# A graph layer's neighbour counts: two buffers of 180 nodes in turns with the products, instead of one buffer of 250

## The chip, the cores and the metric

One core of a Trainium2 chip runs the whole layer. The metric is the device time of one execution in microseconds (us). Engines are called PE (TensorE; PEld is its weight load), DVE (VectorE), ACT (ScalarE), POOL (GpSimd) and SP (SyncE, which here only issues DMAs).

## The reference, cut to what matters

There are N = 6250 nodes with D = 128 values each, and E = 206250 edges, sorted by destination (`dst`). Every edge also has 128 values of its own.

```python
msg = x[src] + edge_attr
agg = jax.ops.segment_sum(msg, dst, num_segments=N)
h = jax.nn.relu(agg @ W1 + b1) @ W2 + b2
# whole-tensor norm, norm over nodes, gelu, + x, then a layer norm of each row
```

The sum splits in two: the edges' own values, summed by destination, and `x[src]`, summed by destination. The second is a product: `agg[n] += sum_s counts[s, n] * x[s]`, where `counts[s, n]` is how many edges run from node s to node n.

## The kernel before, in words

**Stages.** (1) Set-up: `dst` and `src` are read, packed into one list in HBM (`listed`), and turned into small tables; `x` is split into two fp32r parts, `x_hi` and `x_lo`. (2) Lead rounds: groups of 3072 edges are summed by PE. (3) The chunk loop, which also sums the other groups. (4) A tail: two small matrix products per 250 nodes (`up` L740, `down` L750), the norms, and the output.

**Sums of edges.** There are 67 full groups and a rest. A group is loaded by SP in two halves of 768 KB each (L345). DVE makes one-hots for each half (`mark`, L875), PE does 24 recorded matmuls of 128 columns with 32-column weights per half (`sum_half`, L622), ACT copies the sums (`copy_sums`, L489), PE turns them (`turn_sums`, L636), and DVE adds them to `agg` (`add`, L892). Before: 8 lead rounds of 2 groups; then 2 groups in each of 25 chunks. There are 4 buffers for halves.

**Chunks.** A chunk is 250 destination nodes, taken as 125 pairs. POOL gathers for each pair the words of `listed` in which the pair's edges begin (L429, twice 128 words), DVE finds the first edge (`stage_row`, L942 to L946), POOL gathers 128 words from there (L434), DVE makes two tables from them (`make_keys`, L953 to L967), PE turns these (`turn_keys`, L656) and ACT copies them (`copy_keys`, L499). From the turned tables DVE makes marks in bf16, one batch of 25 pairs at a time, 5 batches in a chunk and 3 buffers of marks (`mark_batch`, L982, two instructions each, on 26 pairs with the padding). One matmul per pair (L672, 128 by 98) multiplies its marks into counts; 5 pairs fill a PSUM bank, 25 banks make a chunk, 3 banks go in a ring. ACT copies each bank into `counts` (L519). After the last bank of the chunk comes the product: for each of 49 tiles of nodes, `x_hi` and then `x_lo` as 128 by 128 weights and 250 columns of `counts` (L693, 98 matmuls), summed in one bank; DVE adds that to `agg` (`add_chunk`, L1034).

**Order.** Each engine runs its own list of instructions in order, and semaphores tie them. There is one buffer of counts: PE waits for ACT's last copy before the product, and ACT waits for the product before the next chunk's first copy. PE's list for chunk c is: 25 banks, with a half of a group after banks 2, 8, 14 and 20 and the next chunk's `turn_keys` after bank 20; then 98 product matmuls.

```python
if k == KEYS_AT:                                  # PE, KEYS_AT = 20
    pe.wait_ge(keys_ready, c * 2 + 2)
    turn_keys(c + 1)                              # waits for make_keys(c + 1)
...
pe.wait_ge(banks_free, (c + 1) * BANKS)
```

DVE's list for chunk c is: `stage_tile(c+1)`, batches 0, 1, 2 with the one-hots and the add of the first group between them, `add_chunk(c-1)`, `stage_row(c+1)`, batch 3, the second group, batch 4, `make_keys(c+1)`. A batch waits until the banks of the batch that had its buffer are counted (`banks_done`).

Of the kernel before, what the change touches and what calls it, by code (L numbers as in the profile page):

```python
# [14 lines left out]
P = 128  # L15
# [5 lines left out]
PER = 6  # L21
# [5 lines left out]
HALVES = 4  # L27
PLACES = 4
GPC = 2
HPC = 2 * GPC  # L30
# [11 lines left out]
CHUNK = 250  # L42
PAIRS = CHUNK // PAIR
BATCH = 25
BATCHES = PAIRS // BATCH
BP = BATCH + 1
INTER = 2
BLOCKS_B = BP // INTER
MARKED = 3
# [3 lines left out]
CREDIT = BPB + 1  # L53
RING = 3
# [4 lines left out]
KEYS_AT = 20  # L59
BURSTS = (2, 8, 14, 20)  # L60
SUMS_AT = (11, 23)
BELOW = 3
SEARCH = 13
# [7 lines left out]
def gnn_kernel(nc, x, src, dst, edge_attr, W1, b1, W2, b2, ln_w, ln_b, gn_w, gn_b, gn_ms, out):  # L71
# [11 lines left out]
    CHUNKS = N // CHUNK  # L83
    LEAD = (FULL // GPC) - CHUNKS
    LEAD0 = 2
    EVEN = GROUPS // 32 * 32
    assert D == P and 0 < REST < SUB and REST_P * PER == REST and GROUPS <= 96 and FULL == (LEAD + CHUNKS) * GPC + 1
    assert G_REST_E > G_HALF and EVEN < FULL
    assert CHUNKS * CHUNK == N and CHUNKS % 2 == 1 and LEAD > LEAD0 + 3
# [4 lines left out]
    assert PIECE * (LEAD - 1) == NT  # L94
# [5 lines left out]
    NPAIR = N // PAIR  # L100
    ROWS = E // STRIDE + 1
    LISTED = (ROWS - 1) * STRIDE + P
    assert N <= 1 << DST_SHIFT and 0 < LISTED - E <= P and LISTED % STRIDE == 0 and (ET * SPAN + P) // STRIDE < ROWS and STRIDE == 1 << 4
# [5 lines left out]
    with ExitStack() as ctx:  # L109
# [6 lines left out]
        def sem(name):  # L116
            return ctx.enter_context(nc.semaphore(name))


        edges = sb("edges", [P, HALVES, HALF * D])  # L120
# [4 lines left out]
        LW = P * BP  # L125
        KW = KEYS * BP
        pool_m = sb("pool_m", [P, max(2 * NT * D, MARKED * (LW + KW))], BF16)
        mark_lo = [pool_m[:, s * (LW + KW):s * (LW + KW) + LW].rearrange("p (b v r) -> p b v r", v=P, r=INTER)
                   for s in range(MARKED)]
        mark_key = [pool_m[:, s * (LW + KW) + LW:(s + 1) * (LW + KW)].rearrange("p (b v r) -> p b v r", v=KEYS, r=INTER)  # L130
                    for s in range(MARKED)]
        x_raw = pool_m[:, 0:2 * NT * D].bitcast(F32)
        xs = x_raw.rearrange("p (t d) -> p t d", d=D)
        behind = pool_m[:, 2 * NT * D:MARKED * (LW + KW)]
        below = behind[:, 0:BELOW * SEARCH * PAIRS].rearrange("p (s v) -> p s v", s=BELOW)

        behind_f = behind.bitcast(F32)
        lnstats = behind_f[:, 0:6 * NT].rearrange("p (t s) -> p t s", s=6)
        lnmean, lngap, rstd = [behind_f[:, k * NT:(k + 1) * NT] for k in (6, 7, 8)]
        lnmean_act = behind_f[:, 9 * NT:10 * NT]  # L140
        stats = behind_f[:, 10 * NT:10 * NT + 6 * CHUNKS].rearrange("p (c s) -> p c s", s=6)
        listing = sb("listing", [P, NPAIR + 7], BF16)
        pair_row = listing[:, :].bitcast(I16)
        values = listing[:, 0:P * INTER].rearrange("p (a v r) -> p a v r", a=1, r=INTER)
# [9 lines left out]
        place = sb("place", [P, 2, SPREAD])  # L154
# [7 lines left out]
        hidden = onehot[:, :, :].rearrange("p s e -> p (s e)")[:, 0:2 * HC * CHUNK].rearrange(  # L162
            "p (u k n) -> p u k n", u=2, k=HC)
        gelu = behind_f[:, 10 * NT + 6 * CHUNKS:10 * NT + 6 * CHUNKS + 2 * BLOCK * P].rearrange("p (u n) -> p u n", u=2)
# [9 lines left out]
        pair_i = sb("pair_i", [P, CHUNKS + 1], I32)  # L174
        pair_f = sb("pair_f", [P, CHUNKS + 1])
        pair_w = sb("pair_w", [P, CHUNKS + 1])
        tile_end_i = sb("tile_end_i", [P, SETS], I32)
        tile_end = sb("tile_end", [P, SETS])
        tile_f = sb("tile_f", [P, CHUNKS + 1])
        tile_rows = sb("tile_rows", [P, CHUNKS + 1, 2], I32)  # L180
        tile_slot = sb("tile_slot", [P, 2], I32)
# [9 lines left out]
        hi_i = sb("hi_i", [P, P], I32)  # L191
# [5 lines left out]
        turned_lo = sb("turned_lo", [P, BATCHES, BP], BF16)  # L197
        turned_key = sb("turned_key", [P, BATCHES, BP], BF16)
# [16 lines left out]
        eps = [b[:, 0:D] for b in banks[3:5]]  # L215
        turned_sum = [b[:, D:D + SPREAD] for b in banks[3:5]]
        turn_ps, sps = banks[6], banks[7]
# [3 lines left out]
        ops = [banks[4], sps, banks[0], banks[1]]  # L221
# [40 lines left out]
        pads_ready = sem("pads_ready")  # L262
# [73 lines left out]
        def _(sp):  # L336
# [11 lines left out]
            with sp.Fori(0, LEAD + CHUNKS) as r:  # L348
                for u in range(HPC):
                    load(r * GPC + u // 2, u % 2, u, r * HPC + (u + 1))  # L350
            for k in range(2):
                load(FULL - 1, k, k, 2 * (FULL - 1) + k + 1)
            sp.wait_ge(halves_free, 2 * FULL + 2)
            for k in range(2):
                sp.dma_start(edges[0:REST_P, 2 + k, 0:HP], edge_rest[:, k * HP:(k + 1) * HP]).then_inc(tail_loaded, 16)
# [47 lines left out]
        def _(pool):  # L403
            pool.iota(iota_i[:, :], [[1, P]], base=0, channel_multiplier=0)
            pool.iota(prow_i[:, :], [[0, 1]], base=0, channel_multiplier=1)
            pool.iota(pair_i[:, :], [[PAIR * PAIRS, CHUNKS + 1]], base=0, channel_multiplier=PAIR)
# [3 lines left out]
            for at, to in ((0, half), (half, NPAIR + 7)):  # L410
                pool.iota(pair_row[:, at:to], [[1, to - at]], base=at, channel_multiplier=0,
                          allow_small_or_imprecise_dtypes=True).then_inc(pair_row_ready, 1)
            for s, places in ((halves_free, HALVES), (sums_copied, 3), (sums_turned, 3), (edges_added, 2),
                              (banks_done, CREDIT), (chunk_summed, 1), (chunk_added, 1)):
                pool.sem_inc(s, places)
# [3 lines left out]
            pool.wait_ge(below_ready, 2 * SETS)  # L419
            pool.iota(listing[:, 0:P * INTER], [[1, P], [0, INTER]], base=0, channel_multiplier=0,  # L420
                      allow_small_or_imprecise_dtypes=True).then_inc(pads_ready, 1)


            with pool.Fori(0, CHUNKS + 1) as c:
# [3 lines left out]
                for k in range(2):  # L428
                    pool.indirect_dma_start(begins[0:PAIRS, k * P:(k + 1) * P], None, listed_rows,  # L429
                                            bass.IndirectOffsetOnAxis(tile_slot[0:PAIRS, k:k + 1], 0)  # L430
                                            ).then_inc(begins_loaded, 16)
# [18 lines left out]
        def _(act):  # L450
# [40 lines left out]
            def round_copies(r):  # L491
                for j in range(GPC):
                    copy_sums(r * GPC + j, j)

            def copy_keys(c):
                act.wait_ge(marks_ready, c * BATCHES)
                act.wait_ge(keys_turned, c + 1)
                for at, to in ((LO0, turned_lo), (KEY0, turned_key)):
                    nc.scalar.copy(to[:, :, 0:BATCH], turn_ps[:, at:at + PAIRS].rearrange("p (b n) -> p b n", n=BATCH)  # L499
                                   ).then_inc(keys_ready, 1)  # L500

            for g in range(LEAD0 * GPC):
                copy_sums(g, g % GPC)
            with act.Fori(LEAD0, LEAD - 2) as r:
                round_copies(r)
            act.wait_ge(pads_ready, 2)
            act.wait_ge(keys_turned, 1)
            for at, to in ((LO0, turned_lo), (KEY0, turned_key)):
                nc.scalar.copy(to[:, :, 0:BATCH], turn_ps[:, at:at + PAIRS].rearrange("p (b n) -> p b n", n=BATCH)
                               ).then_inc(keys_ready, 1)  # L510
            for r in range(LEAD - 2, LEAD):
                round_copies(r)
# [739 lines left out]
```

## Time and profile before

| | |
|---|---|
| median of 3 runs | 911.76 us (906.98 to 913.2) |
| profiled execution, its own time | 911.31 us |
| span of the profiled execution | 909.3 us |
| PE busy, PEld busy | 729.4 us (80%), 633.5 us (70%) |
| DVE busy, ACT busy, POOL busy | 678.4 us (75%), 383.4 us (42%), 145.4 us (16%) |
| mean granted TensorE clock | 0.959 |

The busy times are shares of the whole span and mix stages with different limits; what a change in the chunk loop is worth is read from one chunk. Times of instructions and stretches below are counted from the first instruction. The clock is given as a share of full speed: 1.00 is 2.4 GHz and 0.50 is 1.2 GHz. The span ends 2.0 us short of the execution's own time.

### The profile page before, as it was taken

The numbers are of one execution on the slowest core, as the hardware profiler recorded it, in microseconds if no ns is written. First come the engines' busy times: TensorE is split into PE (matmuls) and PEld (weight loads), VectorE is DVE, ScalarE is ACT, GpSimd is POOL, SyncE is SP. The second block draws the span as 40 slices with busy tenths as digits, with TensorE's granted clock in tenths as the row PEclk, the third lists the DMA queues.
The fourth block names the chain that finished last, engine by engine and source line by source line (L and its number), as shares of the span: only waits on it lengthen the run. The fifth ranks groups of instructions, "written<-read, shape, count | busy, mean of one in ns | idle before, by whom it ended". The sixth has DMA issues, their size and how long they took to land.

```text
span 909.3 us, 25887 instructions
## 1 busy us (share of the span) xinstructions
PE 729.4 (80%) x9449; PEld 633.5 (70%) x9449; DVE 678.4 (75%) x1185; ACT 383.4 (42%) x841; POOL 145.4 (16%) x91
## 2 busy tenths in 40 slices
PE   3486569888988888988889988889988889989950
PEld 2464448777877777877777877777877777877830
DVE  5844777877878877878877878877878877844576
ACT  0200034355433555433554433554434554424464
POOL 1210022120221220221120221220221220200000
PEclk9987989899999999999999999999999999999975
DMA  6669973443334443334444334443334444303004
GB/s 173 228 216 361 360 262 99 124 147 115 104 100 121 147 144 116 106 97 125 147 144 114 107 94 128 147 144 112 109 93 130 147 144 113 94 25 141 0 1 141
DMA packets 89477, 123.25 MB, mean 136 GB/s; under 512 B 9029, under 2 KB 85018, under 8 KB 89260
## 3 DMA queue, kind: packets, MB, share of 16 engines
q1 hardware_dynamic: 78992, 112.83, 39.9%
q0 software_dynamic: 6240, 5.08, 2.1%
q10 hardware_dynamic: 4228, 5.12, 1.8%
q8 instruction: 10, 0.16, 0.1%
q14 instruction: 7, 0.05, 0.0%
HBM read 118.91 MB, written 4.03 MB: 135 GB/s over the span
## 4 chain that ended last, share of the span: by engine, by line
PE 48%; DVE 26%; issue 11%; DMA 7%; ACT 5%; DVEq 2%; ACTq 1%; POOL 0%; SPq 0%; POOLq 0%
PE bank L693 33%; DVE pool_m L982 12%; DMA edges<-in_edge_attr_dram 5%; PE bank L622 3%; PE bank L672 3%; ACT counts L519 3%; DVE onehot L875 3%; PE bank L740 3%; PE bank L750 2%; PE bank L656 1%; PE bank L636 1%; DMA agg<-in_dst_dram 1%; DMA begins<-listed,tile_slot 1%; DVE node_f L965 1%; DVE node_f L957 1%
## 5 line engine op out<-in xcount | busy, mean ns | idle before, releaser
L519 ACT CAST counts<-bank 128x490 fp32r<-128x490 f32 x625 | 318.3, 606 | 324.0 <-PE bank L672 324.0
L693 PE MATMUL bank<-counts,x_hi 128*128 128x250 f32 x1225 | 293.5, 284 | 29.6 <-ACT counts L519 29.6
L693 PE MATMUL bank<-counts,x_lo 128*128 128x250 f32 x1225 | 290.6, 281 | 0.0
L982 DVE TENSOR_TENSOR pool_m<-listing,turned_lo 128x3328 bf16<-128x3328 bf16 x125 | 236.7, 1893 | 30.1 <-PE bank L672 26.7
L693 PEld LDWEIGHTS bank<-counts,x_hi 128*128 128x128 f32 x1225 | 234.8, 192 | 33.4 <-ACT counts L519 33.4
L672 PE MATMUL bank<-pool_m 128*128 128x98 bf16 x3125 | 211.2, 210 | 33.0 <-ACT counts L519 22.7
L693 PEld LDWEIGHTS bank<-counts,x_lo 128*128 128x128 f32 x1225 | 235.2, 192 | 0.0
L672 PEld LDWEIGHTS bank<-pool_m 128*128 128x128 bf16 x3125 | 161.9, 99 | 77.6 <-ACT counts L519 75.2
L982 DVE TENSOR_TENSOR pool_m<-listing,turned_key 128x2548 bf16<-128x2548 bf16 x125 | 184.5, 1476 | 0.0
L622 PE MATMUL bank<-edges,onehot 128*32 128x128 f32 x3228 | 126.7, 293 | 30.1 <-DMA edges<-in_edge_attr_dram 23.3
L429 POOL DMA_INDIRECT begins<-listed,tile_slot x52 | 101.9, 1959 | 297.1 <-DVE tile_slot L935 265.2
L622 PEld LDWEIGHTS bank<-edges,onehot 128*32 128x32 f32 x3228 | 88.8, 116 | 46.7 <-issue 20.7
L434 POOL DMA_INDIRECT begins<-listed,row_slot x26 | 33.0, 1270 | 310.6 <-DVE row_slot L946 298.4
L875 DVE TENSOR_TENSOR onehot<-iota_f,dst_cols 128x384 f32<-128x384 f32 x136 | 74.5, 550 | 1.1 <-PE bank L622 0.9
L1034 DVE TENSOR_TENSOR agg<-agg,bank 128x250 f32 (+1 forms) x25 | 10.4, 416 | 75.4 <-PE bank L693 74.6
L489 ACT COPY sums<-bank 128x128 f32<-128x128 f32 x68 | 20.2, 297 | 85.0 <-PE bank L622 85.0
L892 DVE TENSOR_TENSOR agg<-agg,bank 128x128 f32 x68 | 19.0, 280 | 39.4 <-PE bank L636 38.3
L595 PE MATMUL bank<-ones_b,pool_m 128*125 128x1 bf16 x175 | 19.2, 245 | 23.1 <-DVE pool_m L826 23.1
L595 PEld LDWEIGHTS bank<-ones_b,pool_m 128*125 128x125 bf16 x175 | 19.0, 229 | 23.3 <-DVE pool_m L826 23.3
L636 PE MATMUL bank<-place,sums 128*128 128x128 f32 x136 | 34.7, 339 | 0.4 <-ACT sums L489 0.4
L636 PEld LDWEIGHTS bank<-place,sums 128*128 128x128 f32 x136 | 21.2, 197 | 14.9 <-issue 14.0
L546 ACT ACTIVATE onehot<-bank,b1c 128x250 f32<-128x250 f32 x50 | 20.7, 466 | 25.3 <-PE bank L740 25.3
(149 smaller groups left out, 407.9 us busy)
## 6 DMA issues: line engine op xcount, KB each, us to landing
edges<-in_edge_attr_dram SPq DMA_DIRECT2D x134, 768.0 KB, 4.5
out_dram<-pool_m SPq DMA_DIRECT2D x6, 512.0 KB
begins<-listed,tile_slot POOLq DMA_INDIRECT x52, 4.2
agg<-in_dst_dram SPq DMA_DIRECT2D x1, 768.0 KB
agg<-in_src_dram ACTq DMA_DIRECT2D x1, 768.0 KB
listed<-agg ACTq DMA_DIRECT2D x1, 768.0 KB
begins<-listed,row_slot POOLq DMA_INDIRECT x26, 4.3
w<-in_L_gnn_W_dram ACTq DMA_DIRECT2D x2, 128.0 KB, 2.2
```

The costliest lines, as they stand in the source:

```text
L429: pool.indirect_dma_start(begins[0:PAIRS, k * P:(k + 1) * P], None, listed_rows, bass.IndirectOffsetOnAxis(tile_slot[0:PAIRS, k:k + 1], 0) ...
L434: pool.indirect_dma_start(near[0:PAIRS, :], None, listed_rows, bass.IndirectOffsetOnAxis(row_slot[0:PAIRS, 0:1], 0)).then_inc(near_loaded, 16)
L519: nc.scalar.copy(counts[:, :, k * nodes:(k + 1) * nodes].rearrange("p q (i m) -> p q i m", m=PAIR), cps[k % RING][:, 0:nodes * NT].rearran ...
L546: nc.scalar.activation(hidden[:, u, c, :], zps[u][:, c, 0:CHUNK], ACT.Relu, bias=b1c[:, c:c + 1]).then_inc(hidden_ready, 1)
L595: last = nc.tensor.matmul(turn_ps[0:PAIRS, c:c + 1], below[:, i % BELOW, at:at + PAIRS], ones_b[:, :], start=(c == 0 and i == 0), stop=(i ...
L622: last = nc.tensor.matmul(eps[s][b * WINDOW:(b + 1) * WINDOW, :], oh[:, t, :], edges[:, u, t * D:(t + 1) * D], start=(k == 0 and j == 0), ...
L636: nc.tensor.matmul(turned_sum[s], sums[:, :], place[:, s, :], start=True, stop=True).then_inc(sums_turned, 1)
L672: last = nc.tensor.matmul(cps[k % RING][:, i * KEYS:(i + 1) * KEYS], mark_lo[b % MARKED][:, n // INTER, :, n % INTER], mark_key[b % MARKED ...
L693: last = nc.tensor.matmul(sps[:, 0:CHUNK], part[:, q, :], counts[:, q, :], start=(q == 0 and part is x_hi), stop=(q == NT - 1 and part is ...
L740: last = nc.tensor.matmul(zps[u][:, k, 0:CHUNK], w1[:, k * P:(k + 1) * P], agg[:, bass.ds(c * CHUNK, CHUNK)], start=True, stop=True, skip_ ...
L875: dve.tensor_tensor(oh, window, of.to_broadcast([P, HALF, WINDOW]), ALU.is_equal).then_inc(onehot_ready, 1)
L982: last = dve.tensor_tensor(to[b % MARKED], values[:, :, 0:n, :].to_broadcast([P, BLOCKS_B, n, INTER]), of.to_broadcast([P, BLOCKS_B, n, IN ...
```

## The change

A chunk is 180 nodes (90 pairs, 3 batches of 30, 18 banks), so there are 35 chunks, and `counts` has two buffers. PE now goes bank by bank: it counts bank k of chunk c and then does the products of 3 tiles (6 matmuls, 180 columns) of chunk c-1, from bank 2 on (16 times 3 tiles, and one more tile at bank 17). The product's sums have a bank each for odd and even chunks. The ring of count banks has 2 instead of 3, there are 2 buffers of marks instead of 3, and 3 of edge halves instead of 4. The set-up's tables lie in the buffers of counts. Groups go 3 to a round of two chunks: a chunk has three halves, after banks 3, 9 and 15. There are 5 lead rounds of 3 groups. `turn_keys` of the next chunk comes after bank 2 instead of bank 20. Tables are prepared one chunk further ahead, and one gather of 256 words takes the place of two of 128. Chunk 0 is counted alone and the product of chunk 34 comes alone at the end. The tail keeps its 250 columns (`UP`).

```diff
-HALVES = 4
-PLACES = 4
-GPC = 2
+HALVES = 3
+PLACES = 3
+GPR = 3
...
-CHUNK = 250
+CHUNK = 180
-BATCH = 25
+BATCH = 30
-MARKED = 3
+MARKED = 2
-CREDIT = BPB + 1
-RING = 3
+RING = 2
+CREDIT = (MARKED - 1) * BPB + 1
+AHEAD = 2
-KEYS_AT = 20
-BURSTS = (2, 8, 14, 20)
-SUMS_AT = (11, 23)
+KEYS_AT = 2
+BURSTS = (3, 9, 15)
+SUMS_AT = ((11,), (5, 17))
+FIRST_Q = 2
+PER_SLOT = 3
...
-        counts = sb("counts", [P, NT, CHUNK], F32R)
+        counts = sb("counts", [P, 2, NT, CHUNK], F32R)
...
+            def multiply(par, qs):
+                for q in qs:
+                    for part in (x_hi, x_lo):
+                        last = nc.tensor.matmul(sps[par][:, 0:CHUNK], part[:, q, :], counts[:, par, q, :],
+                                                start=(q == 0 and part is x_hi), stop=(q == NT - 1 and part is x_lo))
+                if qs[-1] == NT - 1:
+                    last.then_inc(chunk_summed, 1)
+
+            def count_chunk(c, par, r, first_u):
                 for k in range(BANKS):
                     b = k // BPB
                     if k % BPB == 0:
                         pe.wait_ge(marks_ready, c * BATCHES + (b + 1))
-                    if k >= RING:
-                        pe.wait_ge(banks_free, c * BANKS + (k + 1 - RING))
+                    pe.wait_ge(banks_free, c * BANKS + (k + 1))
                     for i in range(BANK):
...
                     if k == KEYS_AT:
                         pe.wait_ge(keys_ready, c * 2 + 2)
                         turn_keys(c + 1)
+                    if r is None:
+                        continue
+                    if k == FIRST_Q:
+                        pe.wait_ge(banks_free, c * BANKS + RING)
+                        pe.wait_ge(chunk_added, c)
+                    if k >= FIRST_Q:
+                        at = (k - FIRST_Q) * PER_SLOT
+                        multiply(1 - par, range(at, NT if k == BANKS - 1 else at + PER_SLOT))
+                    if k in BURSTS:
+                        u = BURSTS.index(k) + first_u
+                        g = r * GPR + u // 2
+                        begin_half(g, u % 2, edge_loaded[u % HALVES], r * 32 + (u // HALVES * 16 + 16))
+                        sum_half(u, u // 2, u % 2)
+                        if u % 2 == 0:
+                            turn_sums(g - 1, (u // 2 - 1) % GPR)
...
+            def mark_batch(c, par, b):
                 if b == 0:
                     dve.wait_ge(keys_ready, c * 2 + 2)
+                dve.wait_ge(banks_done, c * BANKS + ((b + 1 - MARKED) * BPB + CREDIT))
...
+            def prepare(c, par, r, half, summed):
...
+                mark_batch(c, par, 0)
+                edge_half(0)
+                mark_batch(c, par, 1)
                 make_keys(c + 1)
+                stage_tile(c + 2)
+                edge_half(1)
+                mark_batch(c, par, 2)
+                edge_half(2)
+                stage_row(c + 2)
...
+            with dve.Fori(1, ROUNDS) as it:
+                prepare(it * 2 + 1, 1, it + LEAD, 0, it * 2 - 1 + AHEAD)
+                add_chunk(it * 2 - 1, 1, it * GPR + (g0 - 1))
+                prepare(it * 2 + 2, 0, it + LEAD, HPR // 2, it * 2 + AHEAD)
+                add_chunk(it * 2, 0, it * GPR + g0)
```

`banks_done` starts at `CREDIT` (7), `banks_free` at `RING` (2), `chunk_added` and `chunk_summed` at `AHEAD` (2), so the numbers in these waits are that much above the real counts. `edge_half(i)` is one `mark` with the `add` (first half of a group) or the `put` of the place row (second half).

## Rows read from the trace of the kernel before

**Rows 1.** The page: the chain that ended last, by line.

```profile
PE bank L693 33%; DVE pool_m L982 12%; DMA edges<-in_edge_attr_dram 5%; PE bank L622 3%; PE bank L672 3%; ACT counts L519 3%; DVE onehot L875 3%; PE bank L740 3%; PE bank L750 2%; PE bank L656 1%; PE bank L636 1%; DMA agg<-in_dst_dram 1%; DMA begins<-listed,tile_slot 1%; DVE node_f L965 1%; DVE node_f L957 1%
```

**Rows 2.** Engines by stretch: a product, then counts, then the next product.

```profile
core 0: us, PE busy (x) PEld busy (x) DVE busy (x) ACT busy (x) POOL busy (x), PEclk, DMA share, GB/s
...
294.90:310.60 15.70, 12.29 (x229) 9.39 (x227) 12.96 (x26) 13.04 (x29) 2.57 (x2) 1.00 0.68 202
310.60:322.20 11.60, 11.51 (x98) 11.50 (x98) 9.11 (x9) 0.04 (x1) 2.63 (x2) 1.00 0.05 14
```

**Rows 3.** The page's groups: count, busy us, mean ns | idle before, releaser.

```profile
L519 ACT CAST counts<-bank 128x490 fp32r<-128x490 f32 x625 | 318.3, 606 | 324.0 <-PE bank L672 324.0
```

**Rows 4.** Timeline of TensorE at a product's start and at its last matmul.

```profile
310.69 0.19 PEld L693 LDWEIGHTS bank<-counts,x_hi 128*128 128x128 f32 x1 [1.33 <-ACT counts L519]
310.80 0.19 PEld L693 LDWEIGHTS bank<-counts,x_lo 128*128 128x128 f32 x1
310.91 0.29 PE L693 MATMUL bank<-counts,x_lo 128*128 128x250 f32 x1
...
322.11 0.28 PE L693 MATMUL bank<-counts,x_lo 128*128 128x250 f32 x1
```

**Rows 5.** Timeline of TensorE in the tail: fp32 weights, one column.

```profile
867.44 0.19 PEld L768 LDWEIGHTS bank<-st,ones 128*128 128x128 f32 x1 [2.47 <-DVE st L1137]
...
867.55 0.19 PEld L768 LDWEIGHTS bank<-st,ones 128*128 128x128 f32 x1
```

**Rows 6.** Timeline: 15 count matmuls; a half of a group with its turn.

```profile
299.98 0.87 PE L672 MATMUL bank<-pool_m 128*128 128x98 bf16 x15
...
302.35 0.86 PE L622 MATMUL bank<-edges,onehot 128*32 128x128 f32 x24
303.14 0.49 PE L636 MATMUL bank<-place,sums 128*128 128x128 f32 x2
303.47 0.30 PE L672 MATMUL bank<-pool_m 128*128 128x98 bf16 x3
```

**Rows 7.** Timeline: a batch of marks, the keys, the turn.

```profile
302.09 1.88 DVE L982 TENSOR_TENSOR pool_m<-listing,turned_lo 128x3328 bf16<-128x3328 bf16 x1
303.89 1.47 DVE L982 TENSOR_TENSOR pool_m<-listing,turned_key 128x2548 bf16<-128x2548 bf16 x1
305.29 0.21 DVE L953 TENSOR_SCALAR lo_i<-begins 125x128 int32<-125x128 int32 x1
...
307.66 0.33 PE L656 MATMUL bank<-ident,lo_f 125*128 125x125 f32 x1 [0.97 <-DVE junk L967]
...
307.93 0.86 PE L672 MATMUL bank<-pool_m 128*128 128x98 bf16 x15
```

**Rows 8.** Engines by stretch: TensorE idle, then the work behind it.

```profile
70.60:73.30 2.70, 0.05 (x4) 0.08 (x8) 0.13 (x1) 0.27 (x1) 0.00 (x0) 1.00 1.06 376
73.60:77.00 3.40, 3.13 (x46) 2.03 (x37) 1.44 (x4) 0.01 (x1) 0.00 (x0) 0.50 1.04 365
127.80:133.60 5.80, 0.00 (x0) 0.00 (x0) 4.70 (x9) 1.09 (x3) 1.98 (x1) 0.83 0.44 153
133.60:138.40 4.80, 4.79 (x59) 3.88 (x59) 4.73 (x10) 2.11 (x5) 0.00 (x0) 0.50 0.36 101
818.70:820.90 2.20, 0.04 (x1) 0.04 (x1) 0.58 (x2) 0.00 (x0) 0.00 (x0) 1.00 0.00 0
821.10:824.50 3.40, 3.40 (x9) 2.74 (x9) 0.00 (x0) 0.93 (x3) 0.00 (x0) 0.50 0.53 158
```

**Rows 9.** Timeline of a product at the 1.2 GHz level.

```profile
170.43 0.41 PE L693 MATMUL bank<-counts,x_hi 128*128 128x250 f32 x1
170.64 0.41 PE L693 MATMUL bank<-counts,x_lo 128*128 128x250 f32 x1
```

**Rows 10.** Timeline: group 14's last half; the last product matmul.

```profile
113.64 0.86 PE L622 MATMUL bank<-edges,onehot 128*32 128x128 f32 x24 [0.81 <-DMA edges<-in_edge_attr_dram]
...
813.62 0.28 PE L693 MATMUL bank<-counts,x_lo 128*128 128x250 f32 x1
```

More of the change, by code:

```diff
@@ L141, in gnn_kernel @@
[L141 to L144, printed above, removed]
+        LW = P * BATCH
+        KW = KEYS * BATCH
+        marks = sb("marks", [P, MARKED, LW + KW], BF16)
+        mark_lo = [marks[:, s, 0:LW].rearrange("p (b v r) -> p b v r", v=P, r=INTER) for s in range(MARKED)]
@@ L214, in gnn_kernel @@
         cps = banks[0:RING]
-        eps = [b[:, 0:D] for b in banks[3:5]]
-        turned_sum = [b[:, D:D + SPREAD] for b in banks[3:5]]
-        turn_ps, sps = banks[6], banks[7]
+        eps = [b[:, 0:D] for b in banks[2:5]]
+        turned_sum = [b[:, D:D + SPREAD] for b in banks[2:5]]
+        turn_ps = banks[6]
+        sps = [banks[7], banks[5]]
         KEY0, LO0 = 0, P
@@ L892, in add, with round_groups @@
                 dve.tensor_tensor(at, at, turned_sum[s], ALU.add).then_inc(edges_added, 1)
-            def round_groups(r, first=False, batches=0):
-                for j in range(GPC):
-                    mark(r * GPC + j, 0, j)
+            def round_groups(r, first=False, between=()):
+                for j in range(GPR):
+                    mark(r * GPR + j, 0, j)
                     if not first:
-                        add(r * GPC + (j - GPC), j, base_of(r * GPC + (j - GPC)))
-                    mark(r * GPC + j, 1, j)
-                    put(r * GPC + j, j)
-                    if j < batches:
-                        mark_batch(0, j)
+                        add(r * GPR + (j - GPR), j, base_of(r * GPR + (j - GPR)))
+                    mark(r * GPR + j, 1, j)
+                    put(r * GPR + j, j)
+                    if j < len(between):
+                        between[j]()
             def split_x(i):
@@ L998, in _ @@
-            dve.wait_ge(pads_ready, 2)
-            round_groups(LEAD - 1, batches=2)
-            def head(c, chunks):
-                g = c * GPC + LEAD * GPC
-                stage_tile(c + 1)
-                if chunks is not None:
-                    mark_batch(c, 0)
-                mark(g, 0, 0)
-                base = base_of(g - GPC)
-                if chunks is not None:
-                    mark_batch(c, 1)
-                add(g - GPC, 0, base, chunks)
-                mark(g, 1, 0)
-                put(g, 0)
-                mark_batch(c, 2)
@@ L1016, in rest @@
-            def rest(c, before, groups):
-                g = c * GPC + LEAD * GPC
-                base = base_of(g + (1 - GPC))
-                if before is not None:
-                    add_chunk(before, groups)
-                stage_row(c + 1)
-                mark_batch(c, 3)
-                mark(g + 1, 0, 1)
-                add(g + (1 - GPC), 1, base, c + 1)
-                mark(g + 1, 1, 1)
-                put(g + 1, 1)
-                mark_batch(c, 4)
-                make_keys(c + 1)
@@ new lines, in _, with edge_half @@
+            round_groups(3)
+            split_x(4)
+            split_x(5)
+            stage_row(1)
+            dve.wait_ge(values_ready, 1)
+            round_groups(LEAD - 1, between=(lambda: mark_batch(0, 0, 0), lambda: mark_batch(0, 0, 1)))
+            split_x(6)
+            dve.wait_ge(x_split, NT // PIECE)
+            make_keys(1)
+            stage_tile(2)
+            mark_batch(0, 0, 2)
+            stage_row(2)
+            def prepare(c, par, r, half, summed):
+                def edge_half(i):
+                    u = half + i
+                    g, j, k = r * GPR + u // 2, u // 2, u % 2
+                    mark(g, k, j)
+                    if k == 0:
+                        add(g - GPR, j, base_of(g - GPR), summed)
+                    else:
+                        put(g, j)
+                mark_batch(c, par, 0)
+                edge_half(0)
+                mark_batch(c, par, 1)
+                make_keys(c + 1)
+                stage_tile(c + 2)
[3 more added lines that the diff above has]
+                stage_row(c + 2)
```

332 lines of the change are left out of this document (152 added, 180 removed).

## The prediction

> **What bounds the kernel now.** I read the chain that ended last first: the product line L693 has 33% of it and nothing else has more than 12% [rows 1]. Then one chunk as two stretches: 11.6 us of product, in which PE never rests and ACT does nothing, and 15.7 us of counts, in which ACT is busy 13.0 us, PE 12.3 us and DVE 13.0 us [rows 2]. So the chunk loop is 25 times 27.3 us, in turns: PE alone sets the product, and ACT's copies (606 ns each, 324 us of idle time while PE multiplies, [rows 3]) set the counts with PE close behind. The change wants to lay these two over each other. The two questions are what a product matmul of 180 columns costs, since there are more of them, and what PE, DVE and ACT wait for in the new order.
>
> **The price of a product matmul.** Before there are 25 x 98 = 2450 of 250 columns, after 35 x 98 = 3430 of 180; the columns are the same in sum. From the second matmul's start to the 98th's it is 322.11 - 310.91 = 11.20 us for 96 steps, 0.117 us each [rows 4]. 250 columns at 2.4 GHz are 0.104 us, so columns could be the limit, but two rows say that the fp32 weight load is. At a product's start, where no matmul is ahead, the second load begins 0.11 us after the first [rows 4]. In the tail two loads of such weights with a matmul of one single column also stand 0.11 us apart [rows 5]. So one load holds PE for 0.11 us however few columns follow. The bf16 matmul with equally wide weights steps every (0.86 - 0.21)/14 = 0.046 us, with 98 columns [rows 6], so that load is no bound there. At 180 columns the price lies between 0.11 us (load alone) and 0.117 us (the row of 250 columns); I take 0.115. The product costs 98 x 0.115 = 11.3 us a chunk, as before, and there are ten chunks more: about +113 us of PE work. Below that lies a price by columns, 0.117 x 180/250 = 0.084 us, which is a rival.
>
> The Trainium skill, "TensorE: Matmul & The Clock Gate", section "Back-to-back issue gap", gives a sustained 81 ns per matmul with its load at 128 columns and 131 ns at 512; an estimate from it for 180 columns is 88 ns. By that the sum would lie where the rival "by columns" lies. No row here has fp32 weights of 128 columns faster than 0.11 us, so I side with the rows.
>
> **The new order in PE.** One slot (a bank, then 3 tiles) is 4 steps of 0.046, 0.115 for the first fp32 load, and 6 x 0.115 = 0.99 us. ACT needs 0.606 us for a copy [rows 3] and has two slots, so its work is now covered; were it not, it would cost at most the rest of 0.5 us a bank. A half of a group costs 303.14 - 302.35 = 0.8 us, a turn of sums 303.47 - 303.14 = 0.33 us [rows 6], three halves and on average 1.5 turns a chunk.
>
> **The new wait.** This is what decides. After bank 2 of chunk c PE waits for `turn_keys(c+1)`, that is for `make_keys(c+1)`. In DVE's list this stands behind batch 1 of chunk c. There are two buffers of marks now, and batch 1 of chunk c lies in the buffer of batch 2 of chunk c-1, so it waits for `banks_done` = 18c + 7, less the start value 7: all banks of chunk c-1. So from bank 17 of one chunk there is a chain that no engine can shorten: batch 1 of marks, then the keys, then PE goes on. A batch takes 303.89 - 302.09 = 1.80 and 305.29 - 303.89 = 1.40 us at 26 pairs [rows 7], at 30 pairs 2.08 + 1.62 = 3.7 us. The keys take 307.66 - 305.29 = 2.4 us to PE's first turn [rows 7]. In these 6.1 us PE has only the last 8 product matmuls (0.9 us), banks 0 to 2 (3 x 0.23 us) and about 0.5 us of waiting for ACT's first copy; it then stands for about 4 us in every chunk. Behind PE's wait stand the rest of the products, ACT's keys and bank copies, and so `banks_done` for DVE's batch 2. Before, the same wait comes after bank 20, and PE stands there for 0.97 us [rows 7].
>
> From the keys on PE has: the turn 0.27 (307.93 - 307.66, rows 7), slot 2's products 0.7, slots 3 to 16: 14 x 0.99 = 13.9, halves 3 x 0.8 = 2.4, turns 0.5, bank 17's counts to their landing 0.4: 18.2 us [rows 4, 6, 7]. One chunk is 6.1 + 18.2 = 24.3 us against 27.3 now, but 35 times. Is something later still? DVE has in a chunk 3 batches (11.1), three halves' one-hots with adds (about 3), keys 2.4, gather tables about 1.1, the add of a chunk 0.4: 18 us, with waits for bank 5 (10.5 us after the start of the cycle) and bank 11 (17 us); it is ready for the next batch 1 at 22 us, 2 us early. SP's halves take 4.5 us to land with two chunks' slots of 7 us ahead, POOL has one gather less. These cost nothing while PE's cycle is over 22 us.
>
> **The sum.** Group 14, the last of the lead now, ends near 114.5 us in the trace of before [rows 10]. Two batches stand inside that round, so I put PE's first bank of chunk 0 at 116. Behind it DVE: the last split of x 1.1, keys(1) 2.4, batch 2 from bank 5 on (120.3) 3.7, tables 1.5, batch 0 of chunk 1 3.7, a half 0.9, batch 1 3.7, keys(2) 2.4: PE gets the keys in chunk 1 at about 136 us (131 to 140, as three halves' buffers serve the DMA or not). To the keys of chunk 34 there are 33 cycles of 24.3: 802, so 938; bank 17 at 956; the rest of the product 1; the last product alone 11.3: 968. From the product's end to the end of the span it is 909.3 - 813.9 = 95.4 us now [rows 10], with one more add of 0.3 us after. The sum is 1064 us of span, and 1066 with the 2.0 us between the span and the execution's own time, which itself is 0.4 us below the median of the runs.
>
> **The clock.** In the loop now PE has no idle time above 1.4 us; the clock fell twice near the loop's start (one of the two is in rows 9), else it stays at 1.00 [rows 2]. PE's idle times of over 2 us are elsewhere, and behind each of the three shown (2.7, 5.8 and 2.2 us) the clock stood at 0.50 while PE worked, for 3.4, 4.8 and 3.4 us [rows 8]. At this level a product matmul steps every 0.21 us instead of 0.117 [rows 9], so each us loses 0.45 us: 1.5, 2.2, 1.5, a mean of 1.7 us. The new wait leaves PE idle for 4 us in each of 33 cycles. I expect such a fall in each: 33 x 1.7 = 56 us, between 0 and 33 x 2.2 = 73. With it the forecast is 1066 + 56 = 1122; I say 1120.
>
> In the Trainium skill, "TensorE: Matmul & The Clock Gate", section "What's actually happening", the ramp is put at under 1% of a typical kernel's span. By that the clock would cost some 10 us and the sum would be 1076, which is the rival "the clock holds". The three stretches speak against it for a loop with a wait of 4 us in every turn.
>
> **The rivals.**
> - The clock holds (or falls rarely): 1066 us, 1055 to 1080. For it: much shorter idle times in the loop did nothing. Against it: all three stretches. 17%.
> - A matmul is paid by columns, 0.084 us, and the wait stays: the cycle loses 90 x 0.031 = 2.8 us, 33 x 2.8 = 92 us: 1028 with the falls, 974 without. Against it: [rows 5]. 8%.
> - The wait isn't there, because DVE gets the keys done ahead (I would have the buffers wrong): PE's own work is 18.2 + 0.9 + 0.7 + 0.5 = 20.3 us a chunk, with no idle time and so no fall: 1066 - 33 x 4 = 934 us, 2.5% slower. 6%.
> - The other side: both, no wait and a price by columns. PE has 17.4 us, so DVE's 18 us a chunk sets the loop: 934 - 33 x 2.3 = 858 us, 6% faster. It decides from the point where PE's chunk is below 25 x 27.3 / 35 = 19.5 us, and needs both the order and the row of one column to be misread. 4%.
> - The lay-over does not come about (a copy of ACT or an edge half late in every chunk): each 1 us a chunk is 33 us more, 1150 to 1170. 7%.
>
> **How the numbers follow.** The forecast's own case, 1095 to 1150, has 58%; with the clock's rival below and the late one above, 1040 to 1170 holds some 82% and reaches into the case by columns with falls. A measurement of this kernel can tell about 1% from no change. Faster by over 1%: the last-side case, 0.05. Within 1%: 0.03, for mixtures of the last two sorts. Slower: 0.92.
>
> **What would show it.** Product matmuls of 180 columns stepping at 0.11 to 0.117 us; PE idle before L656's turn for about 4 us in each chunk, released by DVE; key to key in 24 us at full clock and 26 in the mean; granted clock in the loop below 0.95; ACT's idle time before its copies no longer in one piece of 12 us. The prediction is wrong if matmuls step at 0.085 us, if DVE's batch 1 starts before bank 17, or if DVE ends last in the loop.

## The result, and the profile after

The changed kernel takes 1161.55 us (median of 4 runs, 1160.89 to 1162.44), the kernel before 910.08 us in the same comparison: a ratio of 1.2764, with a 95% interval of 1.2713 to 1.2814. It is 28% slower. The forecast was 1120 us, within 1040 to 1170. The direction and the mechanism held; the size is 41 us too small, and the time lies outside the forecast's own case (1095 to 1150). The span of the profiled execution is 1160.0 us.

From the page of after: the engines' busy time, the granted clock in 40 slices, the chain that ended last, and two groups.

```profile
PE 914.3 (79%) x10544; PEld 831.4 (72%) x10544; DVE 701.7 (60%) x1307; ACT 443.7 (38%) x866; POOL 82.6 (7%) x87
...
PEclk9956588888898888889888988888889888987976
...
PE bank L664 36%; PE bank L677 12%; PE bank L623 10%; DVE marks L977 6%; DMA edges<-in_edge_attr_dram 5%; PE bank L637 2%; PE bank L750 2%; PE bank L760 2%; PE bank L652 1%; DMA agg<-in_dst_dram 1%; DVE node_f L964 1%; DVE node_f L956 1%; DVE lo_f L961 1%; DVE node_f L962 1%; PE bank L596 1%
...
L514 ACT CAST counts<-bank 128x490 fp32r<-128x490 f32 x630 | 366.4, 588 | 399.6 <-PE bank L677 398.2
...
L652 PE MATMUL bank<-ident,lo_f 90*128 90x90 f32 x36 | 13.0, 362 | 130.1 <-DVE junk L966 130.1
```

The same clock line on the page of before:

```profile
PEclk9987989899999999999999999999999999999975
```

The product line (L664 now) still leads the chain, the turn of the keys (L652) has 130 us of idle time before it, released by the keys' last instruction on DVE (L966), and the clock line has an 8 almost everywhere in the loop, where before it had a 9. PE's busy time rose by 185 us.

One chunk, DVE's and PE's rows of the timeline of after:

```profile
403.86 2.16 DVE L977 TENSOR_TENSOR marks<-values,turned_lo 128x3840 bf16<-128x3840 bf16 x1 [2.19 <-PE bank L677]
405.94 1.68 DVE L977 TENSOR_TENSOR marks<-values,turned_key 128x2940 bf16<-128x2940 bf16 x1
407.54 0.22 DVE L952 TENSOR_SCALAR lo_i<-begins 90x128 int32<-90x128 int32 x1
...
409.78 0.08 DVE L966 DVE_READ_ACCUMULATOR junk<-junk  x1
409.92 0.30 PE L652 MATMUL bank<-ident,lo_f 90*128 90x90 f32 x1 [3.82 <-DVE junk L966]
...
410.47 0.42 PE L664 MATMUL bank<-counts,x_hi 128*128 128x180 f32 x1
410.69 0.42 PE L664 MATMUL bank<-counts,x_lo 128*128 128x180 f32 x1
```

Batch 1 of the marks starts when PE's bank 17 is done (403.86, after 2.19 us of waiting for L677), takes 2.08 + 1.60 us, the keys take 2.4 us, and 6.1 us after the start PE may go on, having stood for 3.8 us. It is the chain that the prediction wrote down, to a tenth of a microsecond. Over all cycles the idle time before the turn is 3.8 us. Behind it two product matmuls stand 0.22 us apart, twice what they take elsewhere: the clock has fallen. The same chunk by stretch (idle, behind the keys, the rest), and the whole loop:

```profile
core 0: us, PE busy (x) PEld busy (x) DVE busy (x) ACT busy (x) POOL busy (x), PEclk, DMA share, GB/s
405.90:409.90 4.00, 0.20 (x5) 0.04 (x1) 3.61 (x12) 0.79 (x2) 0.00 (x0) 1.00 0.19 71
410.20:417.00 6.80, 6.80 (x56) 6.08 (x54) 0.76 (x2) 1.54 (x4) 0.96 (x1) 0.50 0.16 31
417.00:433.30 16.30, 15.82 (x212) 14.86 (x210) 12.15 (x15) 8.86 (x16) 0.96 (x1) 1.00 0.41 138
171.00:1019.00 848.00, 711.19 (x8481) 660.73 (x8481) 527.84 (x899) 354.49 (x688) 61.23 (x64) 0.88 0.31 94
```

In 6.8 us at 0.50 PE made 56 matmuls, in 16.3 us at 1.00 it made 212, so per us 8 against 13 (the two stretches hold somewhat different mixtures of matmuls). A granted clock of 0.88 over the loop means that about a quarter of it ran at 1.2 GHz. In the trace there is one fall in each of the 33 cycles: 26 last 6.8 us and 7 last 3.4 us. At 2.4 GHz the product steps as forecast, from the timeline of after inside a slot:

```profile
403.08 0.27 PE L664 MATMUL bank<-counts,x_lo 128*128 128x180 f32 x1
403.19 0.27 PE L664 MATMUL bank<-counts,x_hi 128*128 128x180 f32 x1
403.30 0.27 PE L664 MATMUL bank<-counts,x_lo 128*128 128x180 f32 x1
403.42 0.41 PE L677 MATMUL bank<-marks 128*128 128x98 bf16 x5
```

That is 0.11 us for 180 columns, where 250 columns took 0.117 us [rows 4]. ACT's idle time is no longer the price of the product, as it falls into short pieces beside PE's work; it grew, from 324 us [rows 3] to 400 us, of which 398 are waits for PE's count banks, up to 3.3 us each.

### The profile page after: what moved, and what is told of

Same layout as the page of the kernel before. It is cut to its first block, busy times and chain, and to the rows that moved or that the text cites. A ratio compares the mean times of both kernels' runs of the same rounds, so it can differ in the third digit from the quotient of the medians.

```text
span 1160.0 us, 28321 instructions
## 1 busy us (share of the span) xinstructions
PE 914.3 (79%) x10544; PEld 831.4 (72%) x10544; DVE 701.7 (60%) x1307; ACT 443.7 (38%) x866; POOL 82.6 (7%) x87
## 4 chain that ended last, share of the span: by engine, by line
PE 68%; DVE 15%; issue 8%; DMA 6%; ACT 1%; DVEq 1%; ACTq 0%; SPq 0%
PE bank L664 36%; PE bank L677 12%; PE bank L623 10%; DVE marks L977 6%; DMA edges<-in_edge_attr_dram 5%; PE bank L637 2%; PE bank L750 2%; PE bank L760 2%; PE bank L652 1%; DMA agg<-in_dst_dram 1%; DVE node_f L964 1%; DVE node_f L956 1%; DVE lo_f L961 1%; DVE node_f L962 1%; PE bank L596 1%
## 5 line engine op out<-in xcount | busy, mean ns | idle before, releaser
L514 ACT CAST counts<-bank 128x490 fp32r<-128x490 f32 x630 | 366.4, 588 | 399.6 <-PE bank L677 398.2
L664 PE MATMUL bank<-counts,x_hi 128*128 128x180 f32 x1715 | 485.7, 313 | 0.0
L664 PE MATMUL bank<-counts,x_lo 128*128 128x180 f32 x1715 | 453.1, 294 | 0.0
L977 DVE TENSOR_TENSOR marks<-values,turned_lo 128x3840 bf16<-128x3840 bf16 x105 | 226.7, 2159 | 311.6 <-PE bank L677 309.6
L664 PEld LDWEIGHTS bank<-counts,x_lo 128*128 128x128 f32 x1715 | 362.9, 212 | 0.0
L664 PEld LDWEIGHTS bank<-counts,x_hi 128*128 128x128 f32 x1715 | 361.1, 211 | 0.0
L677 PE MATMUL bank<-marks 128*128 128x98 bf16 x3150 | 266.6, 219 | 16.9 <-ACT counts L514 15.6
L677 PEld LDWEIGHTS bank<-marks 128*128 128x128 bf16 x3150 | 178.3, 104 | 42.2 <-ACT counts L514 24.9
L977 DVE TENSOR_TENSOR marks<-values,turned_key 128x2940 bf16<-128x2940 bf16 x105 | 176.7, 1683 | 0.0
L652 PE MATMUL bank<-ident,lo_f 90*128 90x90 f32 x36 | 13.0, 362 | 130.1 <-DVE junk L966 130.1
L652 PEld LDWEIGHTS bank<-ident,lo_f 90*128 90x128 f32 x36 | 5.9, 164 | 135.7 <-DVE junk L966 135.3
L435 POOL DMA_INDIRECT begins<-listed,tile_slot x37 | 35.6, 961 | 503.3 <-DVE tile_slot L935 503.3
L596 PEld LDWEIGHTS bank<-ones_b,over_first 128*90 128x90 bf16 x245 | 19.2, 200 | 23.9 <-DVE over_first L836 23.9
```

Of the source, the lines that this page charges most:

```text
L435: pool.indirect_dma_start(begins[0:PAIRS, :], None, listed_rows, bass.IndirectOffsetOnAxis(tile_slot[0:PAIRS, 0:1], 0)).then_inc(begins_lo ...
L514: nc.scalar.copy(counts[:, par, :, k * nodes:(k + 1) * nodes].rearrange("p q (i m) -> p q i m", m=PAIR), cps[k % RING][:, 0:nodes * NT].re ...
L596: last = nc.tensor.matmul(turn_ps[0:PAIRS, c:c + 1], below[:, i % BELOW, at:at + PAIRS], ones_b[:, :], start=(c == 0 and i == 0), stop=(i ...
L652: last = nc.tensor.transpose(turn_ps[:, at:at + PAIRS], rows[0:PAIRS, :], ident[0:PAIRS, 0:PAIRS])
L664: last = nc.tensor.matmul(sps[par][:, 0:CHUNK], part[:, q, :], counts[:, par, q, :], start=(q == 0 and part is x_hi), stop=(q == NT - 1 an ...
L677: last = nc.tensor.matmul(cps[k % RING][:, i * KEYS:(i + 1) * KEYS], mark_lo[(par + b) % MARKED][:, n // INTER, :, n % INTER], mark_key[(p ...
```

## The experiments

Times are medians; the ratio is to the kernel before, timed on the same chip. Late keys and bf16 products together are `late_bf16`; `_tail` adds the change to the last load.

| kernel | us | ratio, 95% interval | us from keys to keys | clock in the loop |
|---|---|---|---|---|
| before | 910.08 | 1 | 27.5 | 0.99 |
| after | 1161.55 | 1.2764 (1.2713 to 1.2814) | 26.5 | 0.88 |
| keys_late | 940.04 | 1.034 (1.030 to 1.038) | 19.9 | 1.00 |
| keys_first | 942.42 | 1.0359 (1.0316 to 1.0402) | 20.0 | 1.00 |
| wait_filled | 1078.11 | 1.1856 (1.1808 to 1.1903) | 24.0 | 1.00 |
| before_180 | 1106.76 | 1.2171 (1.2082 to 1.226) | 35.3 | 0.73 |
| before_220 | 945.29 | 1.0385 (1.0326 to 1.0444) | 28.8 | 0.92 |
| before_bf16 | 910.66 | 1.0028 (1.0003 to 1.0053) | 27.2 | 0.96 |
| late_bf16 | 888.23 | 0.976 (0.9706 to 0.9813) | 18.6 | 0.97 |
| after_tail | 1152.26 | 1.2672 (1.2604 to 1.274) | 26.5 | 0.88 |
| late_bf16_tail | 877.65 | 0.9634 (0.9589 to 0.968) | 18.6 | 0.97 |

The column "us from keys to keys" is the mean time from one turn of the keys to the next, from the first one inside the loop to the last. The last column is the granted clock of a window over the loop, from 171 us to the last turn.

### The keys late: is the wait what costs?

```diff
-KEYS_AT = 2
+KEYS_AT = 10
```

> The changed kernel with KEYS_AT = 10 instead of 2: nothing else. Theory (the wait for the keys plus the clock's falls behind it): in the trace of after a cycle from keys to keys is 26.5 us in the mean; of this PE's own work at 2.4 GHz is about 19.9 us (18 slots of 0.96, three halves and 1.5 turns of sums 3.1, and the first copy's wait 0.45). Without the wait the falls go too: 1161 - 33 x 6.6 = about 943 us, 925 to 960, with TensorE idle under 1.5 us before the turn and a clock near 1.00 in the loop. Rival (the turns of counts and products are what costs, not the wait): then the wait only moves to the next mark or copy, and the time stays above 1080 us.

Measured: 940.04 us, 19.9 us from keys to keys. Over the loop:

```profile
171.00:808.00 637.00, 622.68 (x8509) 587.73 (x8510) 525.51 (x897) 351.91 (x689) 144.92 (x64) 1.00 0.42 126
```

PE is busy 98% of the loop and the clock is 1.00 throughout. One constant takes 221 us off. The rival, that the wait would only move, is out. Before the turn of the keys PE has no idle time left.

### The keys first: the same from DVE's side

```diff
-                mark_batch(c, par, 1)
                 make_keys(c + 1)
+                mark_batch(c, par, 1)
```

> The changed kernel with make_keys(c+1) ahead of batch 1 in VectorE's list instead of behind it; PE's list is untouched. Theory: the keys then don't stand behind a wait for bank 17, so they are ready when PE comes to bank 2, and the time is that of the late keys, about 943 us (925 to 965). Rival (PE would wait at bank 2 in any case, for the tables' gather or for ACT's copy of the keys): above 1080 us.

Measured: 942.42 us, 20.0 us a cycle, the same as with late keys (the intervals overlap). PE's list is that of after, with its turn behind bank 2; so it is the keys' place behind the wait for bank 17 that cost, and nothing that PE does at bank 2.

### The wait filled: what does the clock cost by itself?

```diff
                         pe.wait_ge(keys_ready, c * 2 + 2)
+                        if r is not None:
+                            for n in range(FILL):     # FILL = 30
+                                nc.tensor.matmul(turn_ps[:, 2 * P:3 * P], x_hi[:, n, :], x_lo[:, 0, :],
+                                                 start=True, stop=True, skip_group_check=True)
                         turn_keys(c + 1)
```

> The changed kernel with 30 matmuls of 128 columns (x_hi as weights, into a part of PSUM that nobody reads) between the wait for the last keys' copy and the wait for the new keys: they take about 30 x 0.11 = 3.3 us of the 4 us in which TensorE stands idle. They compute nothing that is used. Theory (the idle time makes the clock fall): the falls go, the wait stays: a cycle of 23.9 us instead of 26.5, so 1161 - 33 x 2.6 = 1075 us, 1060 to 1095, with the granted clock in the loop at 1.00. Rival (the clock falls because of the light mixture of counts and products, or of power, whatever TensorE does in the wait): 1155 to 1175 us, with half of the falls or more still there.

Measured: 1078.11 us, 24.0 us a cycle; before the turn of the keys about 0.4 us of idle time is left. Over the loop of this kernel:

```profile
171.00:938.00 767.00, 738.15 (x9462) 698.71 (x9461) 529.83 (x906) 354.62 (x688) 61.23 (x64) 1.00 0.35 104
```

With a thousand useless matmuls the kernel is 83 us faster: from 171 us on the clock never falls, and a cycle is 24.0 instead of 26.5 us. The wait is still there, only full, and the mixture of counts and products is unchanged. So the idle time brought the falls, and they cost 2.5 us in each cycle. Together with the late keys this splits the 221 us: 83 us for the clock, 138 us for the wait itself.

### Fewer columns in the kernel before: what sets the step?

```diff
+FEWER = 180
...
-                        last = nc.tensor.matmul(sps[:, 0:CHUNK], part[:, q, :], counts[:, q, :],
+                        m = CHUNK if q == 0 and part is x_hi else FEWER
+                        last = nc.tensor.matmul(sps[:, 0:m], part[:, q, :], counts[:, q, 0:m],
```

> The kernel before, with 97 of the 98 product matmuls of a chunk on 180 instead of 250 columns (the first one keeps 250): the x[src] part of 70 of each 250 nodes is left out almost whole. Theory (the fp32 weight load of 128 columns sets the step, 0.11 to 0.117 us whatever the columns): the product stays at 11 to 11.5 us a chunk and the time at 898 to 912 us. Rival (paid by columns, 0.084 us): 25 x 97 x 0.033 = 80 us less, 832 us.

Measured: 1106.76 us, 198 us slower than the kernel before, with less to compute. Both of my answers missed. The timeline of this kernel, first in a product at 2.4 GHz, then in the next one:

```profile
173.48 0.28 PE L695 MATMUL bank<-counts,x_hi 128*128 128x180 f32 x1
173.59 0.28 PE L695 MATMUL bank<-counts,x_lo 128*128 128x180 f32 x1
173.70 0.27 PE L695 MATMUL bank<-counts,x_hi 128*128 128x180 f32 x1
...
199.90 0.42 PE L695 MATMUL bank<-counts,x_hi 128*128 128x180 f32 x1
200.12 0.42 PE L695 MATMUL bank<-counts,x_lo 128*128 128x180 f32 x1
```

and by stretch, such a product and the counts behind it:

```profile
195.60:219.40 23.80, 23.44 (x133) 23.20 (x137) 10.50 (x15) 1.83 (x4) 2.90 (x2) 0.50 0.04 13
219.40:233.00 13.60, 10.90 (x200) 8.10 (x189) 11.14 (x20) 10.83 (x25) 1.91 (x2) 1.00 0.72 210
```

The step itself is as the theory has it: 0.11 us at 2.4 GHz for 180 columns, against 0.117 for 250. But in 19 of the 25 chunks the product ran at 1.2 GHz from end to end, at 0.21 us a matmul and 20.8 us in all instead of 10.9, though PE was never idle in it. Each of these falls began within 1.1 us before the product's start, so the product it covers did not bring it. PE stands there for 1.2 us for ACT's last copy, as it does in the kernel before; what brought the fall stays open. But the clock came back only 2.2 to 5.4 us after the product's end. With 250 columns, the two falls in the loop of before (one of them in [rows 9]) ended after 6.8 and 3.4 us, inside the product. So the step was confirmed and a second effect found: after a fall, a long row of these short matmuls did not win the clock back.

> The kernel before with 97 of 98 product matmuls of a chunk on 220 columns instead of 250 (30 of each 250 nodes get almost nothing of x[src]). With 180 columns the step was 0.112 us at 2.4 GHz, but the clock stayed at 1.2 GHz through three products of four (1107 us). Theory (a long product keeps or wins back the 2.4 GHz only if its columns fill most of the step; at 250 columns they fill 0.104 of 0.117 us, at 180 0.075 of 0.112): 220 columns, 0.092 of 0.113 us, lie between, with fewer falls than at 180: 900 to 1000 us. Rival (the falls of the 180 columns are a chance of phase between chunk and clock and have nothing to do with the columns): 220 columns may give anything, 900 as well as 1100 us.

Measured: 945.29 us, clock 0.92, cycles of 26.8 to 29.8 us. The loops of before and of this kernel:

```profile
171.00:799.00 628.00, 549.37 (x7450) 482.41 (x7448) 504.27 (x779) 298.05 (x660) 116.89 (x68) 0.99 0.40 120
171.00:832.00 661.00, 581.73 (x7458) 515.26 (x7459) 506.06 (x784) 298.39 (x661) 118.34 (x69) 0.92 0.38 114
```

The time is in the theory's range, and the loop clocks of 0.99, 0.92 and 0.73 at 250, 220 and 180 columns are in its order. But "with fewer falls than at 180" missed: there are 23 falls here, 19 at 180 columns and 2 at 250. What differs is their length: 3.4 or 6.8 us at 220 and 250 columns, 23.9 us at 180 (one of 27.3). The rival, that the falls are a chance of phase, is not excluded for how often they come, and it allowed a time of 945 us as well. Why the clock returned so late at 180 columns stays open.

### bf16 instead of fp32r

```diff
-        counts = sb("counts", [P, 2, NT, CHUNK], F32R)
+        counts_raw = sb("counts", [P, 2, NT, CHUNK], F32)
+        counts = counts_raw[:, :, :, :].bitcast(BF16)[:, :, :, 0:CHUNK]
...
-        x_hi = sb("x_hi", [P, NT, D], F32R)
-        x_lo = sb("x_lo", [P, NT, D], F32R)
+        x_hi = sb("x_hi", [P, NT, D], BF16)
+        x_lo = sb("x_lo", [P, NT, D], BF16)
...
```

This is on top of the late keys; in before_bf16 the three buffers of the kernel before just change their type. In both, the subtraction that makes `x_lo` reads `x_hi` as bf16; its lines are left out above.

> The kernel with the late keys (KEYS_AT = 10), and x_hi, x_lo and the counts in bf16 instead of fp32r (x is split in two bf16 parts; counts are small whole numbers). Theory (the fp32 weight load of 128 columns sets the product's step of 0.112 us at 180 columns): the bf16 load is no bound, as with the count matmuls, so the step falls to about 0.08 us, PE's chunk from 19.9 to about 16.6 us, and VectorE's list becomes the bound, at 19.87 less the 2.1 us that it waited in each cycle of the late keys: 17.8 to 18.3 us. 940 - 34 x 1.8 = about 878 us, 865 to 895, below the kernel before. Rival (the step is not the load's but the matmul's own): no change from 940 us.

Measured: 888.23 us, 2.4% faster than the kernel before (1.9% to 2.9%). From its timeline:

```profile
398.49 0.24 PE L665 MATMUL bank<-counts,x_lo 128*128 128x180 bf16 x1
398.56 0.24 PE L665 MATMUL bank<-counts,x_hi 128*128 128x180 bf16 x1
398.64 0.24 PE L665 MATMUL bank<-counts,x_lo 128*128 128x180 bf16 x1
```

180 columns step every 0.077 us now, which is 180 columns at 2.4 GHz (0.075) and little else. The same matmul in fp32r took 0.112 us, so the floor was that of the type. The run changes weights and columns to bf16 at once; that the floor is the weight load and not the matmul itself rests on the two loads 0.11 us apart in [rows 4] and [rows 5], and no run changes the weights alone. A cycle is 18.6 us, a little over the 17.8 to 18.3 expected. Its waits, from the list over the loop, show why:

```profile
PE bank L678 <- DVE marks L978: 61.4, 53, 2.8
DVE junk L942 <- DMA begins<-listed,tile_slot: 35.3, 16, 2.8
```

PE waits for DVE's marks, as it should where DVE's list is the bound. DVE itself hardly waits for PE any more (4.6 us in the loop), but 35.3 us for gathered tables, 1.1 us a cycle, which the expectation left out. The clock falls again (0.97 in the loop): from 171 us on 10 times, for 3.4 us each, and each fall begins within 2.1 us of the end of an idle stretch of PE of 2.1 to 2.8 us before L678.

> The kernel before with x_hi, x_lo and the counts in bf16 instead of fp32r. Theory: at 250 columns the columns (0.104 us at 2.4 GHz) are nearly as long as the load, so the step goes from 0.117 to 0.109 us only: 25 x 98 x 0.008 = 20 us less, 885 to 895 us. Rival (bf16 is faster by more than the load, or slower by lost clock): under 870 or over 915 us.

Measured: 910.66 us, no gain, against 885 to 895 expected. The step did fall, to about 0.107 us:

```profile
307.87 0.27 PE L693 MATMUL bank<-counts,x_hi 128*128 128x250 bf16 x1
307.98 0.27 PE L693 MATMUL bank<-counts,x_lo 128*128 128x250 bf16 x1
308.08 0.27 PE L693 MATMUL bank<-counts,x_hi 128*128 128x250 bf16 x1
```

So 11 of the 24 cycles take 26.2 or 26.3 us instead of 27.3. But the others take 27.6 to 29.1 us, each with a fall (14 in all, the last product's included, 12 of them of 3.4 us), and the loop's clock is 0.96 where that of before is 0.99. The microsecond gained a chunk was given back to the clock. Why the falls come more often here was not settled: the cycle's length changed along with the matmuls.

### The tail

```diff
-            sp.wait_ge(halves_free, 2 * FULL + HALVES - 1)
+            sp.wait_ge(halves_free, 2 * FULL + 1)
...
-                sp.dma_start(edges[0:REST_P, (2 + k) % HALVES, 0:HP], edge_rest[:, k * HP:(k + 1) * HP]
+                sp.dma_start(edges[0:REST_P, 2, k * HP:(k + 1) * HP], edge_rest[:, k * HP:(k + 1) * HP]
...
-                sum_half(2 + k, 1, k, subs=1)
+                sum_half(2 + k, 1, k, subs=1, slot=2, at=k * HP)
```

In after, PE's timeline behind the last product is:

```profile
1050.76 0.28 PE L664 MATMUL bank<-counts,x_lo 128*128 128x180 f32 x1
...
1052.32 0.86 PE L623 MATMUL bank<-edges,onehot 128*32 128x128 f32 x24
1063.56 1.46 PE L623 MATMUL bank<-edges,onehot 128*32 128x128 f32 x6 [10.38 <-DMA edges<-in_edge_attr_dram]
1064.95 0.80 PE L637 MATMUL bank<-place,sums 128*128 128x128 f32 x2
```

With three buffers of halves the last small load waits for PE's last full group, and PE then waits 10.4 us for the load, and works at half the clock behind it. The load is issued at 1052.0 us, two pieces of 106.5 KB, and little else moves meanwhile:

```profile
1052.10:1063.50 11.40, 1.08 (x26) 0.69 (x25) 2.23 (x11) 0.27 (x1) 0.00 (x0) 0.64 0.06 19
```

A DMA share of 0.06 is as much as one of the 16 engines, at 19 GB/s. So this small load takes 11.5 us, where a half of 768 KB lands in 4.6 us (median).

> The changed kernel with both halves of the rest of the edges loaded into the third buffer of halves (the second half behind the first in it), which is free one group earlier, so that the load doesn't wait for TensorE's last full group. Theory: in the trace of after this load is issued at 1052.0 us, behind the last product, and TensorE stands for 10.4 us for it; then the clock is at 1.2 GHz for 17 us. From the last product to the end it is 109 us, before 95.7 us. With the early load 11 to 14 us go: 1147 to 1151 us. Rival (the tail is longer for another reason, the clock above all): less than 5 us go.

Measured: 1152.26 us, 9.3 us less by the medians, while the span of the profiled execution fell by 12.1 us, from 1160.0 to 1147.9. From the last product matmul to the end it is 98.0 instead of 109.2 us, 11.2 less. The span has the size that was expected; the medians are 2 us short of it.

> The kernel with late keys and bf16 products (888 us) with the same early load of the rest. Theory: the same 11 to 14 us go, 874 to 878 us, the fastest here. Rival: no change, 885 to 890 us.

Measured: 877.65 us, 10.6 us less, 3.7% below the kernel before and the fastest of all.

## Why the prediction was right, and where its size was off

**The price of a product matmul: right.** 0.115 us was taken, 0.112 measured, between the one-column row [rows 5] and the row of 250. The bf16 run shows that the floor comes with fp32r; that it is the load is argued from [rows 4] and [rows 5]. The rival by columns (0.084 us) is out for fp32r. So are the 88 ns estimated from the Trainium skill, "TensorE: Matmul & The Clock Gate", section "Back-to-back issue gap". In bf16 the 0.077 us measured here is below even that.

**The wait: right.** 6.1 us from bank 17 to PE's turn, 3.8 us of idle time for "about 4"; two kernels that take it away in different ways agree within 3 us, at 940 and 942. The prediction put a kernel without the wait at 934 us.

**PE's cycle at full clock: right.** 24.3 us forecast, 24.0 measured with the wait filled.

**The clock: the right mechanism, its term undersized.** The falls came in every cycle. The step that failed in size is "I expect such a fall in each: 33 x 1.7 = 56 us": it measured 26.5 - 24.0 = 2.5 us a cycle, 83 us in all, above even the upper end of 73. The 1.7 came from falls of 3.4 and 4.8 us behind idle time [rows 8]; in after 26 of the 33 falls last 6.8 us and 7 last 3.4, and PE works through 188 us of them in all. At the prediction's own 0.45 us lost per us these are 85 us. So the loss per us was right, and the length of a fall was mis-sized. The rule that I weighed in the Trainium skill, "TensorE: Matmul & The Clock Gate", section "What's actually happening", that the ramp is under 1% of a kernel, is far off for this loop: 83 of 1162 us are 7%. Another section of that page of the Trainium skill, "HAM oscillation — how this bites in real kernels", tells of a kernel whose clock falls behind a wait in every tile, and that is what these traces show.

**The start and the end: too short by 9 and 15 us.** PE has the keys in chunk 1 at 144.8 us instead of 136, since its first bank comes at 126 instead of 116. The prediction took group 14's end from the trace of before, 114.5 us. In after it ends at 126.3: its 30 halves take 2.5 us each where they took 2.1. The stretch from 60 to 120 us, in before, after and after_tail:

```profile
60.00:120.00 60.00, 37.48 (x683) 26.79 (x684) 35.73 (x80) 4.07 (x16) 5.08 (x4) 0.81 1.05 361
60.00:120.00 60.00, 41.52 (x594) 29.39 (x598) 34.07 (x75) 3.26 (x13) 2.87 (x3) 0.59 0.97 315
60.00:120.00 60.00, 39.28 (x602) 27.59 (x602) 35.18 (x77) 3.49 (x14) 3.13 (x3) 0.74 0.98 323
```

DMA moves 315 to 323 GB/s instead of 361. The lower clock is not the main cause: in after_tail, whose lead rounds are the same, it is 0.74 instead of 0.59, and the group still ends at 125.6. The likely cause is that there are three buffers of halves instead of four, which the prediction had named only as an "or"; it is not shown, as no run gives the fourth back. At the end, "with one more add of 0.3 us" left out what fewer buffers do to the last load: from the last product to the end of the span it is 109 us instead of 95.7, of which the tail's run gives 11 back. About 2 of the other 4 us of the 15 are the fall in the last cycle; the rest was not followed. The sum closes: 9 at the start, 33 x (26.5 - 24.3 - 1.7) = 16 in the cycles and 15 at the end are 40 of the 41 us.

**The range: partly luck.** It reached to 1170 us for a rival in which ACT's copies or the edge halves come late in every chunk. That did not happen: in after PE waits 16 us in all for ACT's copies, and in the loop for no edge half. Three terms that were all too small filled the same space.

**The other side: its mechanism exists, with a type changed.** The prediction's fast case has no wait, a price by columns and DVE as the bound, at 858 us. With the late keys and bf16 all three are true, and it takes 888 us; with the early last load 878.

**What the change is worth by itself.** Laying ACT's copies under the product works: PE is busy for 98% of the loop with the late keys. It does not pay, since 35 products instead of 25 are paid at the same floor: 35 cycles of 19.9 are 697 us against 25 x 27.3 = 683. In the traces, from the first count to the last product matmul, it is 701 us with the late keys and 694 in the kernel before, whose first cycles are longer than 27.3. The other 21 us of the difference in span (937.8 against 909.3) lie outside the loop: the first count comes 7.4 us later, and the end is 13.8 us longer, 11 of them the late load.

## What to carry to other kernels

The fp32r product matmul here cost 0.112 us with 180 columns and 0.117 with 250. Look for such a floor in a row with hardly any columns before cutting a tile smaller, since more and shorter matmuls may each cost the same; and then try another type. When the number of buffers falls, write down for each producer which consumer's end it now waits for, and what stands behind it in its own list: here one constant for the place of a step was worth 221 us. A wait of TensorE like this one, 3.8 us in each cycle, is to be counted twice, once as time (138 us here) and once as clock (83 us).

## What the runs showed of the hardware

- In each of 33 cycles an idle stretch of TensorE of about 3.8 us went with a stretch at 1.2 GHz, 26 times of 6.8 us and 7 times of 3.4 us; with 30 useless matmuls in its place the clock stayed at 2.4 GHz, and the kernel was 83 us faster.
- TensorE can be at 1.2 GHz while it never rests: with 180 instead of 250 columns in 97 of 98 product matmuls, a product took 20.8 instead of 10.9 us in 19 of 25 chunks, and the kernel 198 us more. With 220 columns it took 37 us more.
- A step of 128 by 128 fp32r weights took 0.112 us with 180 columns and 0.117 with 250, the same matmul in bf16 0.077 and about 0.107 us.
- A gain of 1 us a chunk in the product of the kernel before (bf16) brought nothing, as the granted clock of its loop went from 0.99 to 0.96.
- A load of two pieces of 106.5 KB with little beside it took 11.5 us at a DMA share of 0.06; loads of 768 KB took 4.6 us each (median).
